# A gated cross-attention and MoE block: rows by transposes, normalisations on VectorE, and four queues in a new order

## The reference

```python
x = x + tanh(g_xattn[0]) * L0_xattn(layernorm(x), fside, ctx)     # x [4, 512, 512]
x = x + tanh(g_ffn[0])   * L0_ffn(layernorm(x), gate_w, w_gate, w_up, w_down, ws_gate, ws_up, ws_down)

def smooth_quant_linear(x, w):                  # L0_xattn: twice for each of 4 batches
    s = sqrt(max(amax(|x|, 0), EPS) / max(amax(|w|, 0), EPS))     # one factor for each column
    xs, ws = x / s, w * s
    x_scale, w_scale = rowmax(|xs|) / 127, rowmax(|ws|) / 127
    x_q, w_q = round(xs / x_scale), round(ws / w_scale)
    return x_q @ w_q.T * x_scale * w_scale.T
gate, up = split(smooth_quant_linear(x, guw)); out = smooth_quant_linear(silu(gate) * up, dw)

# L0_ffn: 2048 tokens, 16 experts of 352 with the top 2 by a softmax router, 256 slots each,
# and a shared expert of 704: y = sum_k topk_w * expert(x) + (silu(x @ ws_gate) * (x @ ws_up)) @ ws_down
```

## Time and profile before

| | us |
|---|---|
| runs | 571.3, 571.96, 572.04; median 571.96 |
| profiled execution, its own time | 572.15 |
| its span | 570.1 |
| PE busy | 541.2 (95%), 3768 instructions |
| DVE busy | 419.4 (74%), 828 |
| ACT busy | 331.3 (58%), 570 |
| POOL busy | 155.4 (27%), 187 |

### The profile page before, as it was taken

One profiled execution on the slowest core, in us unless ns is written; L12 is line 12 of the kernel. 1 busy time (PEld: TensorE's weight loads), 2 busy tenths in 40 slices (PEclk: granted clock), 3 DMA queues, 4 the chain that ended last, 5 costly groups with the idle time before them and its releaser, 6 DMA issues.

```text
span 570.1 us, 10175 instructions
## 1 busy us (share of the span) xinstructions
PE 541.2 (95%) x3768; PEld 459.9 (81%) x3776; DVE 419.4 (74%) x828; ACT 331.3 (58%) x570; POOL 155.4 (27%) x187
## 2 busy tenths in 40 slices
PE   7897879999999999999999999999999999999997
PEld 3453438986888788888889999999999999999985
DVE  3777988998899786587576666666666667765785
ACT  3286776686648627423466666666666667752221
POOL 3428790431033101103222111111111100066730
PEclk9989999999999999999999999999999999999999
DMA  7940121013001130113877776666677767556862
GB/s 265 386 145 2 37 107 43 2 38 147 1 2 38 75 102 2 68 57 88 270 254 251 254 241 225 226 225 225 228 237 254 247 216 249 176 160 188 261 216 75
DMA packets 45891, 89.52 MB, mean 157 GB/s; under 512 B 4304, under 2 KB 24784, under 8 KB 44832
## 3 DMA queue, kind: packets, MB, share of 16 engines
q1 hardware_dynamic: 40736, 72.26, 37.8%
q0 software_dynamic: 5120, 16.78, 9.2%
HBM read 72.25 MB, written 16.78 MB: 156 GB/s over the span
## 4 chain that ended last, share of the span: by engine, by line
PE 57%; DVE 23%; ACT 8%; POOL 6%; issue 5%; DMA 1%; DVEq 0%; SPq 0%; POOLq 0%; ACTq 0%
PE ps_gu L1866 9%; PE ps_gu L1867 9%; PE ps_gu L1868 9%; PE ps_d L1866 6%; PE ps_d L1868 5%; PE ps_d L1867 5%; PE ps_a L2120 3%; POOL w L492 2%; POOL sw_lo L508 2%; PE ps_gu L2427 1%; DVE bn_b L1101 1%; PE ps_d L1887 1%; DMA raw_gu<-in_L_ffn_w_up 1%; ACT y L760 1%; DVE x L1323 1%
## 5 line engine op out<-in xcount | busy, mean ns | idle before, releaser
L1866 PE MATMUL ps_gu<-ex_xhi,w_hi 128*128 128x256 f32 x352 | 99.5, 283 | 0.7 <-DVE wb L1461 0.5
L1867 PE MATMUL ps_gu<-ex_xlo,w_hi 128*128 128x256 f32 x352 | 99.5, 283 | 0.0
L1868 PE MATMUL ps_gu<-ex_xhi,w_lo 128*128 128x256 f32 x352 | 99.4, 282 | 0.0
L1866 PEld LDWEIGHTS ps_gu<-ex_xhi,w_hi 128*128 128x128 f32 x352 | 67.0, 190 | 3.3 <-issue 0.9
L1867 PEld LDWEIGHTS ps_gu<-ex_xlo,w_hi 128*128 128x128 f32 x352 | 67.1, 191 | 1.7
L1004 ACT ACTIVATE ex_hhi<-ex_hid 128x256 fp32r<-128x256 f32 (+1 forms) x66 | 27.6, 418 | 68.3 <-DVE ex_hid L1724 67.3
L1868 PEld LDWEIGHTS ps_gu<-ex_xhi,w_lo 128*128 128x128 f32 x352 | 67.1, 191 | 0.0
L1866 PE MATMUL ps_gu<-xt_hi,sw_hi 128*128 128x256 f32 x220 | 65.1, 296 | 0.1
L1867 PE MATMUL ps_gu<-xt_lo,sw_hi 128*128 128x256 f32 x220 | 62.0, 282 | 0.0
L1868 PE MATMUL ps_gu<-xt_hi,sw_lo 128*128 128x256 f32 x220 | 62.0, 282 | 0.0
L1866 PE MATMUL ps_d<-wd_hi,ex_hhi 128*128 128x512 f32 (+1 forms) x132 | 54.2, 411 | 1.4 <-DVE ex_hlo L1726 1.0
(11 more groups left out here) (255 smaller groups left out, 1386.7 us busy)
## 6 DMA issues: line engine op xcount, KB each, us to landing
raw_gu<-in_L_ffn_w_gate SPq DMA_DIRECT2D x16, 704.0 KB, 4.4
raw_gu<-in_L_ffn_w_up SPq DMA_DIRECT2D x16, 704.0 KB, 5.9
raw_d<-in_L_ffn_w_down SPq DMA_DIRECT2D x16, 512.0 KB, 7.2
expert_out_scratch<-eo SPq DMA_DIRECT2D x16, 512.0 KB, 7.3
w<-in_fside_BxS2xS SPq DMA_DIRECT2D x4, 1024.0 KB, 5.4
x2n_scratch<-y SPq DMA_DIRECT2D x4, 1024.0 KB, 3.9
...
```

What stands on the lines that cost most here:

```text
L1866: pe.matmul(dst, a_hi, b_hi, start=start, stop=False)
L1867: pe.matmul(dst, a_hi, b_lo, start=False, stop=False)
L1868: return pe.matmul(dst, a_lo, b_hi, start=False, stop=stop)
```

## The change

- `row` uses four transposes instead of four fp32 products; it is called five times for each batch.
- normalise_a(0) and normalise_b(0) go from ScalarE to VectorE, as four tensor_scalar instructions (128x512, times the reciprocal deviation, plus the shift) each. Batches 1 to 3 stay on ScalarE.
- quant_w(0) is split: tiles 0 and 1 on ScalarE (quant_w_first), 2 and 3 on VectorE (quant_w_rest); turn_qw(0, c) waits for both.
- SiLU and the gate's product of batch 0 go in two halves of two tiles.
- The lists of TensorE, ScalarE, VectorE and GpSimd have a new order, to the first expert's tokens. There are 150 fillers instead of 158.
- SP's list and everything after the first expert's tokens stay, but for VectorE's weights_d(0, 0), now after sum_shared(2, 1), and ScalarE's, now just ahead of tokens(0, 0).

What TensorE's lists hold between the turns of y, in shared steps (up, down) and rows:

| stretch | before | after |
|---|---|---|
| logits(0) to turn_y(1, 0) | 15, 9, 5 rows | 15, 10, 5 rows |
| to turn_y(2, 0) | 17, 15, 5 rows | 16, 15, 5 rows |
| to turn_y(3, 0) | 14, 20, 2 rows | 16, 16, 2 rows |
| to the last shared_up | 9, 9 | 8, 12 |

The core of the diff: semaphores, GpSimd's list, ScalarE's new steps and its list, VectorE's, TensorE's.

```diff
+        qw_rest_done, silu_first_done = sem("qw_rest_done"), sem("silu_first_done")
...
     norm_a(0)
     root_a(0)
     scale_w(0)
-    split_gu_lo(0)
     norm_a(1)
-    split_gu_lo(1)
-    norm_a(2)
+    split_d_lo(0)
     root_b(0)
     scale_w2(0)
     root_a(1)
+    scale_w(1)
+    split_gu_lo(0)
+    norm_a(2)
+    split_gu_lo(1)
+    norm_b(0)
     split_gu_lo(2)
-    scale_w(1)
-    split_d_lo(0)
-    norm_b(0)
     split_d_lo(1)
     split_gu_lo(3)
     root_b(1)
+    root_a(2)
     scale_w2(1)
-    root_a(2)
     scale_w(2)
+    norm_b(1)
     norm_a(3)
-    norm_b(1)
     root_b(2)
     root_a(3)
     scale_w2(2)
...
+    def quant_w_first(a):
+        act.wait_ge(w_steps_done[LA], a + 1)
+        for j in range(HALF):
+            last = act.activation(w1[:, j, :], w1[:, j, :], ACT.Copy, bias=MAGIC + LOW16, scale=small[LA]["w_inv"][:, j:j + 1])
+        last.then_inc(qw_done[LA], 1)
...
         act.activation(gated[:], xn[:, :, 0:I2], ACT.Silu).then_inc(silu_done, 1)
+    def silu_half(a, h):
+        t = slice(HALF * h, HALF * h + HALF)
+        for j in range(HALF * h, HALF * h + HALF):
+            emptied_a(act, unit_a(a, A_H + j))
+        act.activation(gated[:, t, :], xn[:, t, 0:I2], ACT.Silu).then_inc(silu_done if h else silu_first_done, 1)
...
-    normalise_a(0)
     tanh()
     copy_s(0)
+    router()
     quant_x(0)
     ints_x(0, 0)
-    quant_w(0)
+    quant_w_first(0)
     ints_x(0, 1)
     copy_w(0)
     ints_w(0, 0)
     ints_w(0, 1)
-    split_gu_hi(0)
-    split_gu_hi(1)
-    router()
     split_d_hi(0)
-    silu_a(0)
+    silu_half(0, 0)
+    silu_half(0, 1)
     abs_w(1)
     normalise_a(1)
     abs_x(1)
+    copy_sb(0)
+    split_gu_hi(0)
+    split_gu_hi(1)
     split_gu_hi(2)
-    copy_sb(0)
     quant_g(0)
+    copy_s(1)
     quant_w2(0)
     ints_g(0)
     copy_wb(0)
-    copy_s(1)
     ints_w2(0)
     quant_x(1)
-    split_d_hi(1)
-    abs_w2(1)
+    quant_w(1)
     ints_x(1, 0)
     ints_x(1, 1)
-    quant_w(1)
-    split_gu_hi(3)
     copy_w(1)
     ints_w(1, 0)
     ints_w(1, 1)
-    normalise_b(0)
+    split_gu_hi(3)
+    split_d_hi(1)
+    abs_w2(1)
...
+    def normalise_a(a):
+        dve.wait_ge(rstd_a_done, 4 * a + 4)
+        for j in range(J):
+            last = dve.tensor_scalar(xn[:, j, :], x2[:, a, j, :], rstd_a[:, a, j:j + 1], shift_a[:, a, j:j + 1], ALU.mult, ALU.add)
+        last.then_inc(xn_done, 1)
+    def normalise_b(b):
+        dve.wait_ge(rstd_b_done, 4 * b + 4)
+        for j in range(J):
+            last = dve.tensor_scalar(y[:, j, :], x2[:, b, j, :], rstd_b[:, j:j + 1], shift_b[:, j:j + 1], ALU.mult, ALU.add)
+        last.then_inc(x2n_done, 1)
+    def quant_w_rest(a):
+        dve.wait_ge(w_steps_done[LA], a + 1)
+        for j in range(HALF, J):
+            last = dve.tensor_scalar(w1[:, j, :], w1[:, j, :], small[LA]["w_inv"][:, j:j + 1], MAGIC + LOW16, ALU.mult, ALU.add)
+        last.then_inc(qw_rest_done, 1)
+    def gate_up_half(a, h):
+        t = slice(HALF * h, HALF * h + HALF)
+        dve.wait_ge(silu_done if h else silu_first_done, 1)
+        last = dve.tensor_tensor(gated[:, t, :], gated[:, t, :], xn[:, t, I2:D], ALU.mult)
+        if h:
+            last.then_inc(gated_done, 1)
     def gate_up(a):
...
+    normalise_a(0)
     amax_w(0, 3)
     amax_x(0, 0)
     amax_x(0, 1)
...
     smooth_a(0)
-    amax_w2(0, 0)
     scale_x(0)
     x_steps(0)
+    amax_w2(0, 0)
+    router()
     w_steps(0)
+    quant_w_rest(0)
     stats_a(1)
...
-    gate_up(0)
+    gate_up_half(0, 0)
+    gate_up_half(0, 1)
+    amax_g(0, 0)
     peaks_w(1)
-    amax_g(0, 0)
     amax_g(0, 1)
...
     scale_x(1)
     x_steps(1)
+    w_steps(1)
     dequant_b(0, 0)
     dequant_b(0, 1)
     dequant_b(0, 2)
     dequant_b(0, 3)
-    w_steps(1)
     add_x(0)
     stats_b(0)
-    stats_a(3)
     dequant_a(1, 0)
+    normalise_b(0)
     dequant_a(1, 1)
     dequant_a(1, 2)
...
     peaks_w2(1)
+    gate_up(1)
     peaks_w(2)
...
         for c in range(C):
-            last = pe.matmul(dst[:, c * P:(c + 1) * P], cols[:, c:c + 1].broadcast_to((P, P)), ident[:], start=True, stop=True)
+            last = pe.transpose(dst[:, c * P:(c + 1) * P], cols[:, c:c + 1].broadcast_to((P, P)), ident[:])
         return last
...
         pe.wait_ge(qw_done[LA], a + 1)
+        if a == 0:
+            pe.wait_ge(qw_rest_done, 1)
         turned_integers(fill_a(unit_a(a, A_QW + c)), w1, (2 * c, 2 * c + 1)).then_inc(full_a, 1)
...
-    keep_busy(23)
+    keep_busy(13)
     turn_w(0, 0)
     keep_busy(1)
     turn_w(0, 1)
-    keep_busy(1)
+    keep_busy(2)
     turn_w(0, 2)
     keep_busy(1)
     turn_w(0, 3)
-    turn_w2(0, 0)
+    keep_busy(6)
     turn_x(0, 0)
     keep_busy(1)
     turn_x(0, 1)
     turn_x(0, 2)
     keep_busy(1)
     turn_x(0, 3)
-    keep_busy(11)
+    turn_w2(0, 0)
+    keep_busy(9)
     row_rs(0)
     keep_busy(1)
     row_s(0)
+    turn_router()
     keep_busy(23)
     turn_qx(0, 0)
-    turn_router()
+    turn_w2(0, 1)
     turn_qx(0, 1)
+    keep_busy(1)
     row_w(0)
-    keep_busy(8)
+    keep_busy(5)
     turn_qw(0, 0)
-    turn_w2(0, 1)
     turn_qw(0, 1)
-    keep_busy(4)
+    keep_busy(5)
     product_a(0, 0)
     product_a(0, 1)
     product_a(0, 2)
     product_a(0, 3)
-    keep_busy(12)
+    keep_busy(8)
     turn_g(0, 0)
     keep_busy(1)
     turn_g(0, 1)
-    keep_busy(4)
+    keep_busy(7)
     turn_peaks_w(1)
-    keep_busy(9)
+    keep_busy(7)
     row_b(0)
-    keep_busy(2)
+    keep_busy(5)
     turn_peaks_x(1)
     keep_busy(14)
     row_rs(1)
     keep_busy(1)
+    row_s(1)
     turn_qg(0)
     row_w2(0)
-    row_s(1)
+    keep_busy(8)
     turn_qw2(0)
-    keep_busy(6)
+    keep_busy(4)
     product_b(0, 0)
     product_b(0, 1)
-    keep_busy(1)
+    keep_busy(8)
     product_b(0, 2)
     keep_busy(1)
     product_b(0, 3)
     turn_qx(1, 0)
     turn_qx(1, 1)
-    keep_busy(9)
+    keep_busy(1)
     row_w(1)
-    keep_busy(5)
+    keep_busy(1)
     turn_qw(1, 0)
-    keep_busy(5)
     turn_qw(1, 1)
     keep_busy(5)
     product_a(1, 0)
     product_a(1, 1)
     product_a(1, 2)
+    keep_busy(2)
     turn_y(0, 0)
     keep_busy(1)
...
-    weights_gu(0, 0, 0)
     top_two(3)
     positions(2)
+    count(3)
     slot_rows(2)
-    count(3)
+    sum_shared(1, 1)
     token_parts(3)
...
     shared_hid(2, 1, 3)
+    weights_gu(0, 0, 0)
+    shared_lo(2, 1, 3)
+    shared_hid(2, 1, 4)
     weights_gu(0, 0, 1)
```

More of the change, by code:

```diff
@@ L1557, in _ @@
             shared_hid(0, 0, 3)
+            x_steps(2)
             shared_lo(0, 0, 2)
-            x_steps(2)
-            shared_hid(0, 0, 4)
-            shared_lo(0, 0, 3)
             w_steps(2)
             dequant_b(1, 0)
+            shared_hid(0, 0, 4)
             dequant_b(1, 1)
-            shared_hid(0, 0, 5)
+            token_parts(0)
+            shared_lo(0, 0, 3)
             dequant_b(1, 2)
@@ L1568, in _ @@
             add_x(1)
+            shared_hid(0, 0, 5)
             stats_b(1)
+            shared_lo(0, 0, 4)
+            stats_a(3)
+            count(0)
+            shared_lo(0, 0, 5)
             peaks_w2(2)
-            shared_lo(0, 0, 4)
             shared_hid(0, 1, 0)
-            token_parts(0)
             dequant_a(2, 0)
+            shared_lo(0, 1, 0)
+            x_lo(1, 0)
             dequant_a(2, 1)
-            count(0)
+            x_lo(1, 1)
+            shared_hid(0, 1, 1)
             dequant_a(2, 2)
-            shared_lo(0, 0, 5)
-            x_lo(1, 0)
-            shared_hid(0, 1, 1)
-            x_lo(1, 1)
+            x_lo(1, 2)
             dequant_a(2, 3)
-            shared_lo(0, 1, 0)
-            x_lo(1, 2)
             x_lo(1, 3)
-            shared_lo(0, 1, 1)
             sum_shared(0, 0)
+            peaks_w(3)
             gate_up(2)
-            peaks_w(3)
-            shared_hid(0, 1, 2)
             top_two(1)
@@ L1614, in _ @@
             shared_lo(0, 1, 4)
+            x_steps(3)
+            shared_hid(1, 0, 0)
+            w_steps(3)
+            dequant_b(2, 0)
             shared_lo(0, 1, 5)
-            shared_hid(1, 0, 0)
-            x_steps(3)
+            dequant_b(2, 1)
             shared_hid(1, 0, 1)
-            dequant_b(2, 0)
-            dequant_b(2, 1)
-            w_steps(3)
             dequant_b(2, 2)
@@ L1641, in _ @@
             dequant_a(3, 2)
-            dequant_a(3, 3)
+            token_parts(1)
             shared_hid(1, 0, 4)
             shared_lo(1, 0, 3)
+            dequant_a(3, 3)
             top_two(2)
@@ L1688, in _ @@
             shared_lo(2, 1, 0)
-            weights_gu(0, 0, 0)
             top_two(3)
             positions(2)
+            count(3)
             slot_rows(2)
-            count(3)
+            sum_shared(1, 1)
             token_parts(3)
-            shared_hid(2, 1, 2)
             add_table(2)
@@ L2225, in _ @@
             turn_qw2(1)
[L2226 removed]
             shared_up(0, 0, 5, 0)
             product_b(1, 0)
[L2229 removed]
+            shared_down(0, 0, 1, 0)
             product_b(1, 1)
```

(24 more changed lines are left out.)

308 lines of the change are left out of this document (150 added, 158 removed).

## The result

The changed kernel takes **569.7 us** (median of 5 runs, 569.07 to 570.56) against 572.04 for the kernel before beside it (571.3 to 573.82): ratio 0.9955, 95% interval 0.9942 to 0.9967. It is faster, by 2.3 us and not by 9, and outside my range of 558.5 to 568.0. The profiled execution took 570.56, its span is 568.5, so of 9.15 us forecast 1.6 came.

The account below looks back on a forecast made before the run. TensorE was taken as full from 90.2 to 266.7 us, after an opening set by a serial chain through VectorE, ScalarE and GpSimd. 572.15 less 6.6 (opening) and 2.55 (middle) gave 563.0 us, range 558.5 to 568.

Parts of the forecast that it names:

- the opening's gain of 6.6 us: Opening: batch 0's turn_y at 77.0 us for 83.7, a gain of 6.6 us (5.6 in 1x mode).
- the forecast's shared start: End of the opening: shared_up(0, 0, 0, 0) starts at 84.4 us, held by GpSimd's splits after norm_b(0).
- The port: normalise_b(0) beside split_gu_lo(2): 1.5 us more until sgu_lo, 0 to 1.5 staying; as rival, 564.5 us, chance 0.07.
- The same at the gate: Batch 0's gate in halves: 2.5 us to turn_g become 1.4; turn_g(0, 0) at 41.8 us for 44.7.
- The tensor_scalar alone: VectorE's normalisation: four tensor_scalars of 128x512 take 1.5 us, 2.5 as the other end.
- The clock: Rival, chance 0.04, slower: each fall of TensorE's clock costs 1.5 us where full; seven give 573.5 us.
- The signs that I had named for being wrong: tensor_scalar 0.6 us or more, turn_y(0, 0) after 79, TensorE idle over 6 us between 84 and 257, clock falling there.
- The middle: Stretches between the turns of y to the last shared_up: 2.4+0.75-0.6 = 2.55 us gained, ends 0 to 5.4.
- First stretch: Middle's start: TensorE's work 1.5 us shorter, but VectorE's list, 93% busy, keeps it at 44.3 us.
- Second: Middle's second stretch: one up and five rows less, 3.65 us of TensorE, of which 2.4 taken as gain.
- Third and fourth: Middle's last two stretches: 0.75 us gained in the third, 0.6 lost in the fourth.
- The quantisation in halves: Opening, batch 0's weights: integers end at 34.6 us for 37.1, but VectorE's list lets through 1.85, not 2.5.

Follow-up runs that it names:

- without the collision: Changed kernel with normalise_b(0) on ScalarE and GpSimd waiting for the gate's product before split_d_lo(0): 567.79 us, ratio 0.9914 to the kernel before.
- the fillers alone: Changed kernel with 20 fillers instead of 2 before turn_y(0, 0): 569.39 us, ratio 0.9947 to the kernel before.
- y on ScalarE: Changed kernel with batch 0's normalise_b(0) back on ScalarE: 567.21 us, ratio 0.9915 to the kernel before.

## Why the prediction was wrong

The direction was right, and the step that failed is **the opening's gain of 6.6 us**. At turn_y it was 3.02, at the first shared matmul 0.49. (By its own terms the forecast's shared start is 75.5+3.6+1.3+3.6 = 84.0 and not 84.4; that changes nothing here.)

- *The port, priced on the wrong side and once.* I wrote that normalise_b(0) falls on split_gu_lo(2) and gave 1.5 us "until sgu_lo, of which 0 to 1.5 stays". GpSimd's four splits lost only 0.5 us (4.13 for 3.60). VectorE's four instructions lost 2.4 (4.32 for 1.91), and they were the chain. Each of the four took 1.12 to 1.15 us for 0.48, so each lost some 0.6 beside splits of 0.9: the loss comes as often as a small instruction is issued. The Trainium skill (SBUF — State Buffer, SBUF: two separate sides) says that whichever starts first has the ports for the whole instruction and the other blocks fully; the trace agrees in kind, as far as VectorE slowed to GpSimd's pace of one split at a time (4.32 us beside 4.13). I had cited it and left out the count.
- *The same at the gate.* Nothing was taken for it: 2.83 us for 1.23. turn_g at 42.87 for 41.8 forecast is this, and without the collision it was 41.72. It was only moved by that, though, to the folds behind.
- *The tensor_scalar alone.* Four take 1.91 us where GpSimd is idle, for 1.5 taken and 2.5 as the upper end: a term mis-sized by 0.4 us.
- *The clock.* It was a rival at 0.04 and "slower". It came true in part, at the one wait that I had lengthened: 2.53 us between turn_y and the shared part. I had read "no fall after 44.7 us, though TensorE idled 10 of the next 45.5" as a reason against; but that was one profile, and the fall in the earlier trace rows itself is absent from every later one. To be looked at was how long TensorE idles at each wait of the new chain. That a fall costs 2.53 us is seen in the profile; in the medians the fillers alone gained 0.3.
- *Sum:* norm_b 0.8 late, the tensor_scalars 2.8 longer than the 1.5 taken, the clock 2.5: 6.1 of the 7.55 us missed. The signs that I had named for being wrong all came: 1.14 us for a tensor_scalar, turn_y(0, 0) after 79, 6.8 us of idle TensorE between 84 and 257, and a low clock there. Not all is explained by the collision and the fall: with both gone from the profile (y on ScalarE) the shared part still starts at 86.31 for 84.4 forecast, and no version came below 567.

**The middle** was forecast at 2.55 and gave 1.72 to the load. Another 0.6 us was lost behind the load, where the lists are the old ones; that stretch took 302.7 to 304.7 us in the sixteen profiles, so 0.6 is scatter as far as is known. It was nearer in sum than in its parts. First stretch: 2.1 gained, forecast 0; "93% busy" was not a bound. Second: 0.9 lost, forecast 2.4 gained; VectorE is busy 53.1 of 56.7 us there and TensorE waits longest, 1.6 us, for a product of hidden values that stands behind a table:

```profile
148.62 1.45 DVE pos_oh L1441 x7
150.07 0.60 DVE amax_w_a L1124
150.67 0.34 DVE sh_hid L1469
151.05 0.38 PE ps_gu L1913
```

(the chain of waits of the changed kernel). Third and fourth: 1.1 gained and 0.6 lost, forecast 0.75 and 0.6. By the experiments neither part works alone: transposes in the old order are worth 0.4 us of the middle, the new order with products -0.5 (177.0 for 176.5), both together 1.7 (one profile each, so the two small ones are no more than "about nothing"). My way, TensorE's saving minus what VectorE forbids, has no place for that.

Right or nearly so were: the rows (0.60 us), TensorE's saving in the middle (5.4 forecast, 4.6 measured between 172.56 busy us with products and 167.94 without), the weights' integers (over at 34.6), the first dequantisation, GpSimd's earlier scaling. The quantisation in halves was rightly held not to give its full 2.5 us; it gave 0.4 at most.
